# Three single banks for the transposed scores and two double banks for the maxima, in a fused two-layer attention and expert kernel

## What is computed

```python
x = x + attn_a(layernorm(x))   # 16 heads of 16, biases, ALiBi, causal
x = x + ffn(layernorm(x))      # 8 experts, top 2, exact gelu, first 1024 rows of x.reshape(-1, 256)
x = x + attn_b(layernorm(x))   # 16 heads of 16, rotary, causal, no bias
x = x + ffn(layernorm(x))

scores = einsum('bhqd,bhkd->bhqk', q, k) * scale + bias   # bias: -slope*|i-j|, -inf above the diagonal
out = einsum('bhqk,bhkd->bhqd', softmax(scores), v)
```

## Time and profile before

| | |
|---|---|
| median of 3 runs | 5017.58 us (5014.88 to 5029.58) |
| the profiled execution | 4995.35 us, its span 4993.3 us |
| mean granted TensorE clock | 0.937 of 2.4 GHz |
| busy, share of the span | PE 89%, DVE 64%, ACT 57%, POOL 16% |
| chain that ended last | PE 75%, DVE 17%, DMA 3% |
| maxima, line 993 | 5120 instructions, 2841.1 us |
| exponentials, line 654 | 5120 instructions, 2383.9 us |

### The profile page before, as it was taken

How to read it: one execution, slowest core, us unless ns; L and a number is a source line. 1 busy time by engine, 2 the same in 40 slices (tenths; PEclk the granted TensorE clock), 3 DMA queues, 4 the chain that set the end, 5 groups by cost and what they waited for, 6 DMA issues and landing times.

```text
span 4993.3 us, 104313 instructions
## 1 busy us (share of the span) xinstructions
PE 4439.3 (89%) x41345; PEld 2500.5 (50%) x41345; DVE 3193.5 (64%) x6547; ACT 2840.7 (57%) x6419; POOL 813.7 (16%) x832
## 2 busy tenths in 40 slices
PE   5998989998999988898989998999989999889876
PEld 3444444444444444445854444454444444444665
DVE  4777777777667776674047777777777677767000
ACT  2466666666666665564246666666666666556311
POOL 3000001110111023320023220233022220110012
PEclk8798999999999998899989999999999999989998
DMA  5122223222232233333543332243133232221443
GB/s 164 40 56 53 50 60 83 70 70 38 65 88 74 38 99 84 84 75 111 185 124 93 86 80 45 79 105 84 39 92 83 73 75 53 49 55 37 144 155 123
DMA packets 238751, 406.81 MB, mean 81 GB/s; under 512 B 29324, under 2 KB 153484, under 8 KB 225164
## 3 DMA queue, kind: packets, MB, share of 16 engines
q1 hardware_dynamic: 235192, 391.76, 30.6%
q0 software_dynamic: 3072, 8.39, 0.6%
HBM read 264.25 MB, written 121.50 MB: 77 GB/s over the span
## 4 chain that ended last, share of the span: by engine, by line
PE 75%; DVE 17%; DMA 3%; issue 2%; SPq 1%; POOL 1%; another core or an unknown queue 1%; ACT 0%; POOLq 0%; DVEq 0%; ACTq 0%
PE ps_acc L806 23%; PE ps_r L757 15%; PE ps_p L780 14%; DVE part_max L993 12%; PE ps_r L843 5%; PE ps_p L890 4%; PE ps_r L879 4%; PE ps_p L786 3%; PE ps_r L847 2%; PE ps_r L851 2%; PE ps_r L763 1%; DVE stats L944 1%; PE ps_r L837 1%; DVE xl L957 1%; DMA hid_f<-rows_by_expert 1%
## 5 line engine op out<-in xcount | busy, mean ns | idle before, releaser
L993 DVE TENSOR_REDUCE part_max<-ps_p 128x1 f32<-128x512 f32 (+3 forms) x5120 | 2841.1, 605 | 1133.7 <-PE ps_p L780 802.1
L654 ACT ACTIVATE probs<-ps_r 128x512 f32<-128x512 f32 (+3 forms) x5120 | 2383.9, 535 | 1369.6 <-PE ps_r L757 718.8
L780 PE MATMUL ps_p<-k_stack,q_stack 52*128 52x512 f32 (+3 forms) x5120 | 1421.0, 422 | 387.9 <-DVE part_max L993 364.1
L806 PE MATMUL ps_acc<-probs,v_head 128*17 128x256 f32 x18432 | 1365.4, 386 | 0.0
L757 PE MATMUL ps_r<-q_stack,k_stack 54*128 54x512 f32 (+3 forms) x5120 | 1201.3, 453 | 16.3 <-ACT probs L654 12.3
L780 PEld LDWEIGHTS ps_p<-k_stack,q_stack 52*128 52x128 f32 x5120 | 679.8, 195 | 669.6 <-DVE part_max L993 618.7
L757 PEld LDWEIGHTS ps_r<-q_stack,k_stack 54*128 54x128 f32 x5120 | 518.3, 190 | 740.6 <-ACT probs L654 467.2
L806 PEld LDWEIGHTS ps_acc<-probs,v_head 128*17 128x17 f32 x18432 | 472.3, 99 | 475.2 <-issue 73.0
L786 PE MATMUL ps_p<-id,mk 64*128 64x64 bf16 x4096 | 361.9, 199 | 0.0
L1068 DVE COPY xf<-ps_p 128x256 f32<-128x256 f32 x60 | 25.5, 425 | 460.6 <-PE ps_p L890 460.6
L843 PE MATMUL ps_r<-xT,wqkv 128*128 128x256 f32 x1024 | 282.9, 404 | 1.9 <-ACT xT L671 1.9
(11 more groups left out here) (90 smaller groups left out, 2102.7 us busy)
## 6 DMA issues: line engine op xcount, KB each, us to landing
probs<-w_dram SPq DMA_DIRECT2D x60, 1024.0 KB, 8.2
q_stack<-parts SPq DMA_DIRECT2D x384, 128.0 KB
k_stack<-parts SPq DMA_DIRECT2D x384, 128.0 KB
parts<-pa SPq DMA_DIRECT2D x128, 256.0 KB, 2.5
parts<-pb SPq DMA_DIRECT2D x128, 256.0 KB, 3.2
o_sums<-acc_sb SPq DMA_DIRECT2D x1024, 17.0 KB
bk<-o_sums SPq DMA_DIRECT2D x64, 256.0 KB
bk<-recips SPq DMA_DIRECT2D x64, 256.0 KB
```

What stands on the lines that cost most here:

```text
L654: act.activation(probs[:, at % PBUF, u, 0:QW - q0], ring(i + u)[:, q0:QW], ACT.Exp)\
L780: mm[u] = pe.matmul(p1_bank(g, n, u)[:, 0:w], qs[s][r, qb * P:(qb + 1) * P], ks[s][r, kc * QW:kc * QW + w], start=True, stop=True)
L806: mm = pe.matmul(ps_acc[tile:tile + DH + 1, first:e % 2 * D + D], v_head[:, beta % 2, kb, 2 * p + u, :], probs[:, at % PBUF, u, lo - q0:to ...
L993: dve.reduce_max(part_max[:, u, qb, kc:kc + 1], p1_bank(g, n, u)[:, 0:w], AX_X).then_inc(p1_used, 1)
```

## The change

1. `ps_r` becomes a ring of three single banks, `ps_p` four banks: two double ones. Unit n takes double bank n % 2, head u in its bank u.
2. VectorE takes the maximum of both heads in one instruction over the double bank; it waits for both heads' matmuls. TensorE waits once per unit, for the maximum of unit n - 2. The heads of a unit are issued 1, 0.
3. Steps go in pairs. The score of an odd step is issued in two pieces: head 0 ahead of the jobs, head 1 behind the next unit. `ring_uses` and ScalarE's order follow.
4. times_v is called at the end of each pair, with the same lag as before.
5. In the experts `ps_p` and `ps_r` change roles.

```diff
-RING = 4
-P1_RING = 3
+RING = 3
@@ ring_uses
-        for n in range(STEPS):
-            seq += [("s", g, n, 0), ("s", g, n, 1)] + [j for j in JOBS[g][n] if j[0] in RING_JOBS]
+        for n in range(0, STEPS, 2):
+            seq += [("s", g, n, 0), ("s", g, n, 1), ("s", g, n + 1, 0)]
+            seq += [j for j in JOBS[g][n] if j[0] in RING_JOBS]
+            seq.append(("s", g, n + 1, 1))
@@ build
-        ps_p = ctx.enter_context(nc.psum_tensor("ps_p", [P, P1_RING, QW], F32))
+        ps_p = ctx.enter_context(nc.psum_tensor("ps_p", [P, 4, QW], F32))
...
-        def p1_place(g, n, u):
-            return 2 * (STEPS * g + n) + u
+        def p1_banks(g, n):
+
+            return slice(2 * (n % 2), 2 * (n % 2) + 2)
+
+        def block_bank(g, n, u):
+            return ring(PLACE[("s", g, n, u)])
@@ scalar
-                for n in range(STEPS):
-                    exp_block(g, n)
+                for n in range(0, STEPS, 2):
+                    exp_block(g, n, 0)
+                    exp_block(g, n, 1)
+                    exp_block(g, n + 1, 0)
                     for j in JOBS[g][n]:
                         job(*j)
+                    exp_block(g, n + 1, 1)
@@ tensor: score
-            def score(g, n):
+            def score(g, n, heads):
...
-                for u in range(2):
-                    pe.wait_ge(ring_used, i + u - RING + 1)
+                for u in heads:
+                    pe.wait_ge(ring_used, PLACE[("s", g, n, u)] - RING + 1)
@@ tensor: unit
+                if at >= 2:
+                    pe.wait_ge(p1_used, at - 1)
+                banks = ps_p[:, p1_banks(g, n), :]
                 mm = [None, None]
-                for u in range(2):
-                    at = p1_place(g, n, u)
-                    if at >= P1_RING:
-                        pe.wait_ge(p1_used, at - P1_RING + 1)
+                for u in (1, 0):
@@ tensor: the loop
-                for n in range(STEPS):
-                    score(g, n)
+                for n in range(0, STEPS, 2):
+                    score(g, n, (0, 1))
                     if g + 1 < NG:
                         unit(g + 1, n)
+                    score(g, n + 1, (0,))
                     for j in JOBS[g][n]:
                         job(*j)
-                    if n >= PV_LAG and (n - PV_LAG) % 2 == 0:
-                        times_v(g, (n - PV_LAG) // 2)
-                    if n + STEPS == 2 * (GROUPS - 1) + PV_LAG and g % (NG // 2):
+                    if g + 1 < NG:
+                        unit(g + 1, n + 1)
+                    score(g, n + 1, (1,))
+                    if n:
+                        times_v(g, n // 2 - 1)
+                    elif g % (NG // 2):
                         times_v(g - 1, GROUPS - 1)
@@ vector: unit
                 for u in range(2):
                     dve.wait_ge(p1_mm[u], STEPS * g + n + 1)
-                    dve.reduce_max(part_max[:, u, qb, kc:kc + 1], p1_bank(g, n, u)[:, 0:w], AX_X).then_inc(p1_used, 1)
+                dve.tensor_reduce(part_max[:, :, qb, kc], ps_p[:, p1_banks(g, n), 0:w], AX_X, ALU.max)\
+                    .then_inc(p1_used, 1)
```

More of the change, by code:

```diff
@@ L65 @@
 GROUPS = STEPS // 2
-PV_LAG = 3
 LAST_GROUP = {3: 7, 2: 13, 1: 17, 0: 19}
@@ L753, in score @@
                 mm = [None, None]
-                for u in range(2):
-                    pe.wait_ge(ring_used, i + u - RING + 1)
+                for u in heads:
+                    pe.wait_ge(ring_used, PLACE[("s", g, n, u)] - RING + 1)
                     r = slice(HALF * u, HALF * u + ROWS)
-                    mm[u] = pe.matmul(ring(i + u)[:, q0:QW], ks[s][r, kb * P:(kb + 1) * P],
+                    mm[u] = pe.matmul(block_bank(g, n, u)[:, q0:QW], ks[s][r, kb * P:(kb + 1) * P],
                                       qs[s][r, qt * QW + q0:(qt + 1) * QW], start=True, stop=True)
                 for part in range(2 if kb >= 4 * qt else 0):
-                    for u in range(2):
+                    for u in heads:
                         r = slice(HALF * u, HALF * u + HALF)
                         lo = q0 + HALF * part
-                        mm[u] = pe.matmul(ring(i + u)[:, lo:lo + HALF], mk[r, 2 + part, :], id64[r, :], start=False,
-                                          stop=True, skip_group_check=True)
-                for u in range(2):
+                        mm[u] = pe.matmul(block_bank(g, n, u)[:, lo:lo + HALF], mk[r, 2 + part, :], id64[r, :],
+                                          start=False, stop=True, skip_group_check=True)
+                for u in heads:
                     mm[u].then_inc(s_mm[u], 1)
@@ L770, in unit @@
                 qb, kc, w = UNIT[n]
-                s = g % SLOTS
+                s, at = g % SLOTS, STEPS * g + n
                 if n == 0:
                     pe.wait_ge(stack_in[s], stack_count(g))
+                if at >= 2:
+                    pe.wait_ge(p1_used, at - 1)
+                banks = ps_p[:, p1_banks(g, n), :]
                 mm = [None, None]
-                for u in range(2):
-                    at = p1_place(g, n, u)
-                    if at >= P1_RING:
-                        pe.wait_ge(p1_used, at - P1_RING + 1)
+                for u in (1, 0):
                     r = slice(HALF * u, HALF * u + MAX)
-                    mm[u] = pe.matmul(p1_bank(g, n, u)[:, 0:w], qs[s][r, qb * P:(qb + 1) * P],
+                    mm[u] = pe.matmul(banks[:, u, 0:w], qs[s][r, qb * P:(qb + 1) * P],
                                       ks[s][r, kc * QW:kc * QW + w], start=True, stop=True)
                 for part in range(2 if kc == qb // 4 else 0):
-                    for u in range(2):
+                    for u in (1, 0):
                         r = slice(HALF * u, HALF * u + HALF)
                         lo = w - P + HALF * part
-                        mm[u] = pe.matmul(p1_bank(g, n, u)[:, lo:lo + HALF], mk[r, part, :], id64[r, :], start=False,
+                        mm[u] = pe.matmul(banks[:, u, lo:lo + HALF], mk[r, part, :], id64[r, :], start=False,
                                           stop=True, skip_group_check=True)
```

30 lines of the change are left out of this document (14 added, 16 removed).

## The result

| | before | with the change |
|---|---|---|
| time, median of 4 runs | 5016.35 us | **5181.69 us** |
| lowest to highest | 5014.88 to 5029.58 | 5157.00 to 5216.63 |
| ratio, 95% interval | | **1.0327** [1.0297, 1.0358] |
| profiled execution, its span | 4995.35, 4993.3 | 5202.24, 5200.4 |
| mean granted clock of TensorE | 0.937 | 0.905 |

Slower, as forecast, and inside the range, but 67 us above the forecast of 5115. Between the two profiled executions the difference is 207 us, and the working had +97 for it.

A forecast was written before the change was run, and what follows sets the result against it. TensorE and VectorE, handing banks to each other, were taken as the bound, neither alone. Jobs +271 and the rest -174 gave +97: 4995.35 became 5092, and with 22 for the median of runs, 5115 us; range 5030 to 5195.

The forecast's parts named there:

- A job-free pair gains 1.53 - 1.25 = 0.28 and takes 2.66: Attention pairs without a job: TensorE waits until 1.25 for the first exponential, not 1.53 for VectorE; 520 pairs, -146 us.
- It goes at 1.25 where it went at 0.65 ... I take 0.60: A job becomes the ring's fourth use and waits for the first exponential: 0.60 us lost per pair, bounds 0.24 and 0.84.
- The long jobs' three terms: Pairs with long jobs: +182 us for 304, +27 for 72 at diagonal steps or with two jobs, +29 for 30 at step 6.
- 1.22 for the maximum over two banks: VectorE's combined maximum takes 1.22 us against 2 x 0.685; only the 40 units before the loop gain, -3 us.
- Rival 4: A maximum over two banks costs more than the two it replaces; at 1.40 it adds 73 us, 5188; chance 0.06.
- Gaps behind a normalization: 32 steps where TensorE idles 4.61 us for VectorE's first maximum: four banks gain 1.1 each, to some 3.5; -36 us.
- Rival 1: The ring's wait does not bind in job pairs, only the extra slot costs: 4960 us, faster; chance 0.09.
- Rival 2: Shorter gaps spare 28 stretches of TensorE's low clock, -104 us: 5011, no change; chance 0.09.
- moved from 0.937 by more than 0.02: Sign of a wrong prediction: TensorE's mean granted clock leaving 0.937 by more than 0.02.
- Rival 3: A new idle of 0.36 in every job pair costs as many low-clock stretches again, +104 us: 5220; chance 0.06.
- xt jobs, 0.17 each: 96 short xt jobs, said to have both old waits already: estimated 0.17 us each, +16 us.
- The last group, +8: Last group, without units: 20 pairs go from 2.24 to 2.66 us each, +8 us.

The follow-up runs named there:

- experiment 1: Changed kernel with the jobs of a pair moved back ahead of the lone score of head 0, nothing else: 4785.82 us, 0.9615 of the kernel before.
- experiment 4: Changed kernel with one maximum per head again, on the same double banks and in the same order: 5173.27 us, 1.0373 of the kernel before.

## Why the prediction was right, and what in it was wrong

- **"A job-free pair gains 1.53 - 1.25 = 0.28 and takes 2.66"**: right, 2.66 is the median of the trace, and TensorE waits for ScalarE before the lone score.
- **"It goes at 1.25 where it went at 0.65 ... I take 0.60"**: right for the start and the pair's length, 3.95 instead of 3.97; the idle ahead of the job is 0.27 in TensorE's rows, not 0.36. The long jobs' three terms, +238, came out as +260 with the clock in it. That the place of the job is the cause, and not the lone score by itself, experiment 1 shows: the same banks and the same lone score, and 3.9% faster than before. Its -3.85% of 5016 is -193 us, where the prediction's terms without the jobs sum to -174.
- **1.22 for the maximum over two banks**: right (1.223), and its weight too: nothing that could be measured. Rival 4 falls. The Trainium skill, in "TensorEngine Tiling (Array Packing)", section "PSUM Bottleneck", advises to vectorize PSUM access across several tiles of the same bank. Here the two tiles lie in two banks, and one access for both is shorter too (1223 ns against 2 x 685), but experiment 4 gives the time with two to within the intervals.
- **Gaps behind a normalization**: 3.32 where the working had 3.5, from 4.61; right.
- **Rival 1**, a ring wait that doesn't bind, falls with the job's start at 1.25. **Rival 2** too: the gaps did become shorter, but the clock fell.
- **The step that failed: the sum took the clock as it was.** Its durations are those of a full clock at both ends, and the mean clock was left at 0.937. It fell to 0.905, which the prediction itself had named as a sign of being wrong ("moved from 0.937 by more than 0.02"). Time at the low clock, some 630 us there and put at no change, became 988. No term of the sum stands for that; the median lies inside the range because the range was wide enough, and the profiled execution (5202) lies above it.
- **Rival 3** had the direction and about the price (+104, where the low clock is an estimated +140), but only a chance of 0.06; the clock is most of what lies between 97 and 207. Its mechanism, low stretches that the idle in every job pair starts, is not what came: the pairs with a long job ran at full clock as before (17 of 424 touch a low stretch, 23 before), and the number of low stretches stayed at 45. The stretches that were there grew longer, in the xt pairs behind the gaps. Against the rival the prediction argued that stretches with an idle of 0.31 in each pair ran at full clock. They did. That an idle doesn't start a low stretch was taken as evidence that it doesn't prolong one. "TensorE: Matmul & The Clock Gate" of the Trainium skill, on its second failure mode, has small idles between groups of matmuls and a clock that swings. The trace agrees in part: the clock is 0.905 against 0.937 in experiment 1, which differs from the change in the jobs' place alone, but it did not swing more often than in the kernel before (45 low stretches in each).
- **xt jobs, 0.17 each**, was too small by itself: at full clock such pairs take 3.39 against 3.04 (medians), so 0.35, and 96 x 0.35 = +34 instead of +16. The reason given, "they have both old waits already", holds for the waits; but the job and the unit lay inside them and now stand behind the ring's wait one after the other, 0.37 for the job, as the timeline of such a pair has it:

```profile
1392.98 0.19 PEld L760 LDWEIGHTS ps_r<-q_stack,k_stack 54*128 54x128 f32 x2 [0.21 <-ACT probs L654]
...
1394.29 0.20 PEld L840 LDWEIGHTS ps_r<-identf,xl 128*128 128x128 f32 x2 [0.78 <-issue]
1394.66 0.19 PEld L783 LDWEIGHTS ps_p<-k_stack,q_stack 52*128 52x128 f32 x2 [0.17 <-issue]
...
1396.35 0.19 PEld L760 LDWEIGHTS ps_r<-q_stack,k_stack 54*128 54x128 f32 x2 [0.42 <-ACT probs L654]
```

The job goes at 1.31, the unit at 1.68, and the pair takes 3.37. Most of the rest of +145 goes with the low clock: 280 us more of it in these pairs, at 0.39 us each an estimated +109.
- **The last group, +8**: +35. It had been priced at full clock; all but one of its pairs ran at the low one.
- Pairs without a job went the other way: with the gaps among them they gained 228 instead of 171. What of it is the gaps' and what the pairs' was not separated.

What stays open: why a low stretch lasts longer when the jobs stand behind the lone score, and why the last group, whose only job is one transposed maximum, fell into one of 75 us. The runs show how much the low time grows with the jobs' place and with the gaps, and not how the chip decides; no run was made on the last group alone, and none without long gaps. The 0.39 us per us at the low clock rests on four runs of one kernel.

## What to carry to other kernels

In a ring of banks used in program order, count the uses: with three banks the fourth in a pair waits for the first one's reader, and what stands there should be the instruction with the most other work ahead of it, not the one with most behind it. Moving one item one place was worth 7.4%, more than banks and combined instruction together (1.0%). A sum made of full-clock durations needs a line of its own for the clock: read where the low stretches begin and end now, and give new waits in the pairs behind them a price. And when work is spread to close a gap, look for who waits for its result: here the gap moved there, from 3.32 to 3.02.

## What the runs showed of the hardware

- The order with the jobs behind the lone score, whose 311 waits of long jobs' weight loads are 0.5 us each on average, goes with 384 us more at 1.2 GHz of some 5000 (988 against 604, the kernel with the change against experiment 1). The kernel before has as many low stretches as the kernel with the change (45), but shorter ones.
- Gaps behind a normalization of 3.8 instead of 4.6 went with the same mean clock, 0.937 (experiment 1 and the kernel before). Spreading the normalization over eleven steps, which left gaps of 2.3 to 3.5 us at the first xt job, raised it in three kernels, by 0.017 to 0.026.
- In the last group of the kernel with the change the clock stayed at 1.2 GHz for 75 us while TensorE was busy 59.94 of 70 us; in the kernel before the same group ran at 2.4 GHz, busy 39.84 of 40 us.
- The kernel with the change was granted between 0.903 and 0.916 in four runs, and its time went with it, from 5217 to 5157.
- One maximum over two PSUM banks of 128 x 512 takes 1223 ns against 2 x 685: 147 ns less, as much as the fixed part of about 150 ns that the rows of 128 and 512 columns give, so the second bank cost nothing that shows.
